# Graph attention with layer norm on one core: the move of transposed probabilities by groups of two slots, 128 KB an issue, from SyncE alone

## The reference

```
q, k, v = heads(x @ Wq + bq), heads(x @ Wk + bk), heads(x @ Wv + bv)
scores  = q @ k.T / 8
probs   = softmax(scores + where(adj, 0, -9e15))
ctx     = probs @ v                      # per head, then heads side by side
y       = x + ctx @ Wf + bf
out     = (y - mean(y)) / sqrt(var(y) + 1e-5)
```

## Time and profile before

| what | value |
|---|---|
| median of three runs | 1729.52 us (1724.23 to 1731.74) |
| the profiled execution, its own time | 1730.58 us |
| its span, first to last instruction | 1728.6 us |
| mean granted PE clock | 0.881 of 2.4 GHz |
| PE busy | 1326.2 us, 77% of the span |
| DVE busy | 1060.2 us, 61% |
| ACT busy | 721.8 us, 42% |
| POOL busy | 655.7 us, 38% |
| mean traffic of the DMA engines | 146 GB/s |

### The profile page before, as it was taken

One profiled execution on the slowest core, in us unless ns is written; L12 is line 12 of the kernel. 1 busy time (PEld: TensorE's weight loads), 2 busy tenths in 40 slices (PEclk: granted clock), 3 DMA queues, 4 the chain that ended last, 5 costly groups with the idle time before them and its releaser, 6 DMA issues.

```text
span 1728.6 us, 29185 instructions
## 1 busy us (share of the span) xinstructions
PE 1326.2 (77%) x8406; PEld 948.2 (55%) x8406; DVE 1060.2 (61%) x1617; ACT 721.8 (42%) x1404; POOL 655.7 (38%) x958
## 2 busy tenths in 40 slices
PE   7777887777877689677897688866887778888773
PEld 5555565545745457455574455644656545565542
DVE  5566665765656656565566765566656567566752
ACT  5444543444434444344443434434443435443430
POOL 2223542444414444154432543325433245333333
PEclk9888898889988889897998888988899889998877
DMA  4556655565455655555555555565555555555552
GB/s 152 141 132 154 159 143 147 150 160 153 121 152 147 163 147 131 147 150 155 147 136 152 149 151 141 138 156 152 149 145 138 154 153 150 153 133 153 149 144 74
DMA packets 184872, 251.61 MB, mean 146 GB/s; under 512 B 52464, under 2 KB 86384, under 8 KB 184688
## 3 DMA queue, kind: packets, MB, share of 16 engines
q1 hardware_dynamic: 147824, 199.06, 44.1%
q10 hardware_dynamic: 36864, 50.38, 11.9%
HBM read 35.33 MB, written 12.58 MB: 28 GB/s over the span
## 4 chain that ended last, share of the span: by engine, by line
SPq 79%; issue 9%; PE 4%; ACT 2%; DVE 2%; DMA 2%; ACTq 1%; POOL 1%; POOLq 0%; DVEq 0%
SPq L301 76%; PE context_ps L519 2%; DMA prob_t<-prob 1%; ACT prob L611 1%; DVE prob L697 1%; ACTq L301 1%; SPq L371 1%; PE score_ps L503 1%; SPq L357 1%; SPq L336 1%; SPq L364 1%; PE job_ps L408 0%; DMA x_in<-in_x_dram 0%; POOL res L294 0%; DVE weight_lo L758 0%
## 5 line engine op out<-in xcount | busy, mean ns | idle before, releaser
L519 PE MATMUL context_ps<-prob_t,v_all 128*64 128x256 f32 x3072 | 468.4, 472 | 239.8 <-DMA prob_t<-prob 239.8
L611 ACT ACTIVATE prob<-prob,row_min 128x1024 f32<-128x1024 f32 x384 | 439.5, 1146 | 500.1 <-DVE row_min L689 433.6
L689 DVE CUSTOM_DVE_ANT_0 prob<-score_ps,mask 128x1024 f32<-128x1024 f32 x384 | 454.3, 1220 | 206.1 <-PE score_ps L503 168.4
L697 DVE STREAM_TRANSPOSE prob<-prob 128x1024 f32<-128x1024 f32 x384 | 457.9, 1231 | 148.9 <-ACT prob L611 148.9
L519 PEld LDWEIGHTS context_ps<-prob_t,v_all 128*64 128x64 f32 x3072 | 294.6, 173 | 413.8 <-issue 298.3
L818 POOL TENSOR_TENSOR diag<-ident,inv_sum 128x512 f32<-128x512 f32 x96 | 99.9, 1040 | 410.5 <-DVE inv_sum L702 408.8
L619 ACT ACTIVATE context_hi<-context 128x256 fp32r<-128x256 f32 x96 | 40.1, 418 | 456.1 <-DVE context L707 285.2
L812 POOL TENSOR_TENSOR q_lo<-raw,q_hi 128x256 fp32r<-128x256 f32 x95 | 69.4, 730 | 351.0 <-ACT raw L603 350.9
L707 DVE TENSOR_TENSOR context<-context_ps,context 128x256 f32<-128x256 f32 x96 | 40.0, 416 | 238.1 <-PE context_ps L519 237.9
L408 PE MATMUL job_ps<-xt_hi,weight_hi 128*128 128x256 f32 (+1 forms) x423 | 149.4, 353 | 26.9 <-ACT raw L601 26.7
L503 PE MATMUL score_ps<-k_hi,q_hi 64*128 64x512 f32 x768 | 145.0, 456 | 21.8 <-DVE row_min L689 16.4
(11 more groups left out here) (72 smaller groups left out, 1717.7 us busy)
## 6 DMA issues: line engine op xcount, KB each, us to landing
prob_t<-prob SPq DMA_DIRECT2D x2304, 64.0 KB, 2.0
prob_t<-prob ACTq DMA_DIRECT2D x768, 64.0 KB, 2.1
res<-in_x_dram SPq DMA_DIRECT2D x32, 384.0 KB, 3.7
out_dram<-res SPq DMA_DIRECT2D x32, 384.0 KB, 2.5
x_in<-in_x_dram SPq DMA_DIRECT2D x30, 384.0 KB, 3.5
adj_in<-in_adj_dram SPq DMA_DIRECT2D x31, 256.0 KB, 2.8
prob_t<-in_L_gnn_Wk_dram SPq DMA_DIRECT2D x1, 576.0 KB, 3.9
prob_t<-in_L_gnn_Wq_dram SPq DMA_DIRECT2D x1, 576.0 KB, 7.8
```

The source lines that it names most:

```text
L519: last = pe.matmul(context_ps[64 * head:64 * head + 64, 0:GQ], v_all[:, kt, col:col + HS], keys, start=(kt == 0), stop=(kt == TT - 1))
L611: nc.scalar.activation(probabilities(t), probabilities(t), ACT.Exp, scale=-1.0, bias=row_min[:, ring:ring + 1], accum_out=row_sum[:, s // ...
L689: nc.vector.tensor_tensor_reduce(probabilities(t), in_quarters(score_ps[:, head, :]), in_quarters(mask[:, s % 2, :]), 1.0, HUGE, ALU.add, ...
L697: nc.vector.transpose(probabilities(t), probabilities(t)).then_inc(squared, 1)
```

## The change

A group is now moved at once, after its second slot. For each pair (a, c) one transfer carries the four units of the group, 128 KB in 32 runs of 4 KB. Sixteen issues a group stand on SP's queue. ACT issues none and no longer waits for the transposes. To make the runs contiguous, the layouts are `prob[P, group, c, slot, head, 256]` with two groups (before: three slots) and `prob_t[P, group, a, slot, head, 256]`. DVE waits for `landed` only in the first slot of a group, and for the group two before.

Other buffers become smaller: `res` has four tiles for eight, `context_hi` and `context_lo` four for six. The order changes with them: the mix of group g stands in slot 2g + 4 for g from 3 on (before: 2g + 3), mixes 0, 1 and 2 in slots 6, 8 and 9 (before 5, 6 and 7), the last two of a batch in the next one's slots 0 and 2. The p jobs, residuals, normalisations, loads and stores are placed anew, and the last batch has one more slot without units.

```diff
-RING = 3
 STEADY = {
-    0: [("k", 2, 0, 0), ("k", 2, 1, 0), ("p", -4, 0, 0)],
-    1: [("q", 2, 0, 0), ("i", -1, 0, 0), ("m", -1, 0, 0)],
-    2: [("p", -3, 0, 0), ("v", 0, 0, 0), ("v", 1, 0, 0)],
-    3: [("v", 2, 0, 0), ("v", 3, 0, 0), ("v", 4, 0, 0)],
-    4: [("q", 0, 1, 0), ("v", 5, 0, 0), ("v", 6, 0, 0), ("v", 7, 0, 0)],
-    5: [("i", 0, 0, 0), ("m", 0, 0, 0), ("q", 1, 1, 0)],
-    6: [("i", 1, 0, 0), ("m", 1, 0, 0)],
-    7: [("i", 2, 0, 0), ("m", 2, 0, 0)],
-    8: [("q", 2, 1, 0), ("p", -2, 0, 0), ("p", -1, 0, 0)],
-    9: [("i", 3, 0, 0), ("m", 3, 0, 0)],
...
+    0: [("q", 1, 0, 0), ("i", -2, 0, 0), ("m", -2, 0, 0)],
+    1: [("q", 2, 0, 0)],
+    2: [("i", -1, 0, 0), ("m", -1, 0, 0)],
+    3: [("v", 0, 0, 0), ("v", 1, 0, 0), ("v", 2, 0, 0)],
+    4: [("q", 0, 1, 0), ("q", 1, 1, 0), ("v", 3, 0, 0), ("v", 4, 0, 0)],
+    5: [("v", 5, 0, 0), ("v", 6, 0, 0), ("v", 7, 0, 0)],
+    6: [("i", 0, 0, 0), ("m", 0, 0, 0)],
+    7: [("q", 2, 1, 0), ("p", -2, 0, 0), ("p", -1, 0, 0)],
+    8: [("i", 1, 0, 0), ("m", 1, 0, 0)],
+    9: [("i", 2, 0, 0), ("m", 2, 0, 0)],
+    10: [("i", 3, 0, 0), ("m", 3, 0, 0)],
+    11: [("q", 0, 2, 0), ("x", 0, 0, 1), ("x", 1, 0, 1), ("x", 2, 0, 1), ("p", 0, 0, 0)],
+    12: [("i", 4, 0, 0), ("m", 4, 0, 0)],
+    13: [("q", 1, 2, 0), ("p", 1, 0, 0)],
+    14: [("i", 5, 0, 0), ("m", 5, 0, 0)],
+    15: [("q", 2, 2, 0), ("q", 0, 3, 0), ("p", 2, 0, 0)],
+    16: [("i", 6, 0, 0), ("m", 6, 0, 0)],
+    17: [("q", 1, 3, 0), ("q", 2, 3, 0), ("x", 0, 1, 1), ("x", 1, 1, 1), ("x", 2, 1, 1), ("p", 3, 0, 0)],
+    18: [("i", 7, 0, 0), ("m", 7, 0, 0)],
+    19: [("k", 0, 0, 1), ("k", 0, 1, 1)],
+    20: [("i", 8, 0, 0), ("m", 8, 0, 0)],
+    21: [("k", 1, 0, 1), ("k", 1, 1, 1), ("p", 4, 0, 0)],
+    22: [("q", 0, 0, 1), ("i", 9, 0, 0), ("m", 9, 0, 0)],
+    23: [("k", 2, 0, 1), ("k", 2, 1, 1), ("p", 5, 0, 0)],
 }
-STORES = {5: -2, 12: -1, 16: 0, 20: 1}
-RES_LOADS = {8: 2, 15: 3, 19: 0, 23: 1}
-X_LOADS = {2: (0, 0), 4: (0, 1), 11: (1, 0), 14: (1, 1)}
-RESIDUALS = {1: 0, 2: 1, 11: 2, 17: 3}
-NORMALISE = {3: -2, 10: -1, 13: 0, 18: 1}
+STORES = {4: -2, 10: -1, 16: 0, 20: 1}
+RES_LOADS = {8: 0, 12: 1, 18: 2, 22: 3}
+X_LOADS = {2: (0, 0), 4: (0, 1), 12: (1, 0), 14: (1, 1)}
+RESIDUALS = {2: -1, 10: 0, 14: 1, 20: 2}
+NORMALISE = {0: -2, 8: -1, 14: 0, 18: 1}
...
-        prob = sb("prob", [P, RING, 4, 2, GQ], F32)
-        prob_t = sb("prob_t", [P, 2, 2, 4, 2, GQ], F32)
+        prob = sb("prob", [P, 2, 4, 2, 2, GQ], F32)
+        prob_t = sb("prob_t", [P, 2, 4, 2, 2, GQ], F32)
...
-        def move_square(queue, s, a, c):
+        def move_square(queue, group, a, c):
-            group, qt, ring = s // 2, s % 2, s % RING
-            queue.dma_start(prob_t[32 * c:32 * c + 32, group % 2, qt, a].rearrange("p h n -> p (h n)"),
-                            prob[32 * a:32 * a + 32, ring, c].rearrange("p h n -> p (h n)")
-                            ).then_inc(landed[ring], 16)
+            queue.dma_start(prob_t[32 * c:32 * c + 32, group % 2, a].rearrange("p q h n -> p (q h n)"),
+                            prob[32 * a:32 * a + 32, group % 2, c].rearrange("p q h n -> p (q h n)")
+                            ).then_inc(landed[group % 2], 16)
...
-            def move(b, s):
-                sp.wait_ge(squared, at(b, UNITS, 2 * s + 2))
-                if s % 2 == 0:
-                    sp.sem_inc(sp_waited, 1)
-                    sp.wait_ge(mixed, at(b, GROUPS, s // 2 + 1))
+            def move(b, group):
+                sp.wait_ge(squared, at(b, UNITS, 4 * group + 4))
+                sp.sem_inc(sp_waited, 1)
+                sp.wait_ge(mixed, at(b, GROUPS, group + 1))
                 for a in range(4):
                     for c in range(4):
-                        if not (a == c):
-                            move_square(sp, s, a, c)
+                        move_square(sp, group, a, c)
...
                 for s in range(SLOTS):
-                    move(b, s)
+                    if s % 2 == 1:
+                        move(b, s // 2)
...
-            def move(b, s):
-                act.wait_ge(squared, at(b, UNITS, 2 * s + 2))
-                if s % 2 == 0:
-                    act.wait_ge(mixed, at(b, GROUPS, s // 2 + 1))
-                for a in range(4):
-                    for c in range(4):
-                        if a == c:
-                            move_square(act, s, a, c)
...
                 if head == 0:
-                    dve.wait_ge(landed[s % RING], at(b, 256 * SLOTS // RING, 256 * (s // RING + 1)))
+                    if s % 2 == 0:
+                        dve.wait_ge(landed[s // 2 % 2], at(b, 128 * GROUPS, 256 * (s // 4 + 1)))
```

More of the change, by code:

```diff
@@ L87, in slot_work @@
     if s >= SLOTS:
-        return LAST_24 if mode == "last" else []
+        return LAST_24 if s == SLOTS else LAST_25
     if mode == "first" and s < 2:
         return FIRST_0 if s == 0 else FIRST_1
-    if mode == "last" and s == 22:
-        return LAST_22
     return [w for w in STEADY[s] if not (mode == "first" and w[1] < 0) and not (mode == "last" and w[3] == 1)]
 def slots_of(mode):
-    return range(SLOTS + 1 if mode == "last" else SLOTS)
+    return range(SLOTS + 2 if mode == "last" else SLOTS)
 MODES = ("first", "mid", "last")
@@ L183, in graph_attention @@
         x_loaded = [sem(f"x_loaded{i}") for i in range(2)]
-        res_loaded = [sem(f"res_loaded{g}") for g in range(4)]
+        x_early = sem("x_early")
+        res_loaded = [sem(f"res_loaded{i}") for i in range(2)]
         adj_loaded = sem("adj_loaded")
@@ L190, in graph_attention @@
         squared = sem("squared")
-        landed = [sem(f"landed{i}") for i in range(RING)]
+        landed = [sem(f"landed{i}") for i in range(2)]
         inverted = sem("inverted")
@@ L213, in graph_attention @@
         pool_waited = sem("pool_waited")
-        stored = [sem(f"stored{g}") for g in range(4)]
+        stored = [sem(f"stored{i}") for i in range(2)]
         def at(b, per, plus):
@@ L284, in probabilities @@
         def probabilities(t):
-            return prob[:, t // 2 % RING, :, t % 2, :]
+            return prob[:, t // 4 % 2, :, t // 2 % 2, t % 2, :]
         def in_quarters(keys):
@@ L292, in scale_rows @@
             for tile in range(2):
-                n = (2 * group + tile) % TT
+                n = (2 * group + tile) % 4
                 engine.tensor_scalar(res[:, n, :], res[:, n, :], mean_var[:, group % 2, tile, 0:1],
@@ L327, in _ @@
             sp.dma_start(bf_rows[:], bf.partition_broadcast(P)).then_inc(bf_in, 16)
+            sp.wait_ge(job_done, 6)
             for g in range(2):
                 sp.dma_start(res[:, 2 * g:2 * g + 2, :], x_tiles[0, :, 2 * g:2 * g + 2, :]).then_inc(res_loaded[g], 16)
-            for i in range(RING):
-                sp.sem_inc(landed[i], 256)
+                sp.sem_inc(landed[g], 256)
             def load_adjacency(b, group):
@@ L382, in body @@
                         store(b, STORES[s])
[L383 to L388, removed]
+                    if s in RES_LOADS and (RES_LOADS[s] >= 2 or b.mode != "first"):
+                        load_residual(b, RES_LOADS[s])
             body(Batch("first", 0, 0))
@@ L396, in _ @@
                 store(last, group)
-            for g in range(4):
-                sp.wait_ge(stored[g], 16 * BATCH)
+            for i in range(2):
+                sp.wait_ge(stored[i], 32 * BATCH)
         @block.tensor
@@ L416, in transpose_x @@
                 for i in range(4):
-                    src = x_in[:, i] if mode != "start" or half == 0 else res[:, 4 + i]
+                    src = x_in[:, i] if mode != "start" or half == 0 else res[:, i]
                     last = pe.transpose(bank[:, i * P:(i + 1) * P], src[:, t * P:(t + 1) * P], ident[:])
@@ L463, in bank_free @@
                 if prior[0] == "p":
-                    assert not back
-                    pe.wait_ge(sum_done, at(b, TT, prior[1] + 9))
+                    pe.wait_ge(sum_done, at(b, TT, prior[1] + 9 - back * TT))
                 else:
@@ L509, in mix @@
                 pe.wait_ge(context_done, at(b, GROUPS, group + 2))
-                for s in (2 * group, 2 * group + 1):
-                    pe.wait_ge(landed[s % RING], at(b, 256 * SLOTS // RING, 256 * (s // RING + 2)))
+                pe.wait_ge(landed[group % 2], at(b, 128 * GROUPS, 256 * (group // 2 + 2)))
                 if group == 0:
@@ L538, in _ @@
                 if n == 3:
-                    for g in (2, 3):
-                        pe.wait_ge(res_loaded[g], 16)
+                    pe.wait_ge(x_early, 16)
                 if n >= 4:
@@ L713, in add_residual @@
                 dve.wait_ge(res_done, at(b, TT, n + 1))
-                nc.vector.tensor_tensor(res[:, n % TT, :], job_bank(b.mode, job)[:, 0:H], res[:, n % TT, :],
+                nc.vector.tensor_tensor(res[:, n % 4, :], job_bank(b.mode, job)[:, 0:H], res[:, n % 4, :],
                                         ALU.add).then_inc(sum_done, 1)
@@ L720, in moments @@
```

(17 more changed lines are left out.)

44 lines of the change are left out of this document (20 added, 24 removed), and 14 rows, old and new, of the table STEADY.

## The result

The changed kernel takes 1501.82 us in the median (1498.75 to 1508.24) against 1727.85 us for the kernel before in the same comparison. The ratio is 0.8696, with a 95% interval of 0.8657 to 0.8735. The forecast was 1490 us. The profiled execution has a span of 1506.3 us at a mean granted clock of 0.916.

The account below looks back on a forecast made before the run. SP's queue, issuing transfers, bounds the kernel. Slots' 161 us plus 6.2, 5.5, 1.3 and 5 make 179 a batch, taken as 180; 27 + 177 + 6 x 180 + 205.6, plus 2, gives about 1490 us (1400 to 1580).

Parts of the forecast that it names:

- Rival D: Whole kernel: nothing changes, as later mixes eat the saving or the chain was misread; 1730 us; 4 in 100.
- The price of an issue: SP's queue: an issue stays at 0.635 us with doubled bytes; a batch costs SP 130 us instead of 191.
- Rival C: SP's queue: an issue's time follows its bytes, 1.27 us each, 252 us a batch, about 2080 us; 4 in 100.
- rival A: DMA: the transfer becomes the limit at 160 GB/s, below the needed 206; a group lands after 15 us; 1570 us; 15 in 100.
- The new sum: Slot-by-slot walk of the new order plus delays: 179 us a batch, taken as 180.
- move(2) behind mix(0): Slot 8: group 2's transfer waits for a mix in slot 6, lands at 15.6 us and delays the slot by 1.3 us.
- diag(3) late: Slots 8 to 10: a normalisation on POOL delays the diagonal that i(3) needs; 22.6 us instead of 17.1, +5.5.
- q(2,2) late: Slot 15: POOL, busy normalising, makes q's low part late for slot 16's scores; slot takes 12.9 us, +6.2.
- other low clock: PE: lower clock after idling costs 2 us a batch outside slot 16, which has 3 us; slot 10's is counted elsewhere.
- Lateness on POOL: POOL works in order, so normalisations delay short jobs: +6.2 us at slot 15 and +5.5 us in slots 8 to 10.
- Rival B: POOL is not late and PE's clock stays up, so only 161 us a batch remain: about 1345 us; 13 in 100.
- the sum without lateness: All slots of a batch, before POOL's delays, the landing delay and low clock are added: 161 us.

Follow-up runs that it names:

- The halves: Changed kernel with each 128 KB transfer cut into two of 64 KB, all 32 a group on SP's queue: 2189.46 us, 1.2702 of the kernel before.
- the old counts in the new order: Changed kernel with 64 KB transfers, 24 a group on SP and 8 on ACT, as before the change: 1779.66 us, 1.0324 of the kernel before.

## Why the prediction was right, point by point

**The bound.** Right, and shown from both sides. SP's queue set the pace. The halves alone bring it back as the chain, at 1.27 of before, and the old counts in the new order land at 1.03. Rival D, no change, is out with the result.

**The price of an issue.** Right: 591 ns for 128 KB as for 64 KB. Rival C is out. A landing of 2.3 us was taken and 2.3 measured, so rival A is out at one queue's rate. It was not far off, though, as the last section tells.

**The new sum.** The first mask stands at 27.8 us (forecast 27). The first batch took 178.3 us (177), the six of the loop 182.5 on average (180), the last with the tail 205.1 (205.6). By slots, for the batch from 941.90 to 1123.26 us:

| slots | forecast, us | measured, us |
|---|---|---|
| 0 to 2 | 17.8 | 15.5 |
| 3 to 6 | 27.2 | 28.2 |
| 7 (move(2) behind mix(0)) | 9.9 | 10.1 |
| 8 to 10 (diag(3) late) | 22.6 | 22.0 |
| 11 | 9.1 | 10.7 |
| 12 | 5.7 | 5.6 |
| 13 | 7.4 | 10.0 |
| 14 | 5.7 | 5.7 |
| 15 (q(2,2) late) | 12.9 | 13.8 |
| 16 | 8.7 | 6.2 |
| 17 | 9.9 | 11.5 |
| 18 to 22 | 32.4 | 31.2 |
| 23 | 7.9 | 11.0 |
| other low clock | 2.0 | in the slots |
| batch | 179.2 | 181.4 |

The total is better than its terms: some came out 11.0 us longer in all and others 8.7 us shorter. That it was met within 2.2 us is in part luck. The batch shown is also a short one, by slot 10: the loop's other batches had 23.4 to 23.6 us in slots 8 to 10. Five terms deserve a word.

*Missed.* "The other buffers and semaphores cost nothing" was wrong. The ring of four context_hi places makes ACT wait for p(1), as the fourth row of the engines' waits shows. Slot 13 took 2.6 us more than forecast, and giving the places back made the changed kernel 1.1% faster.

*Missed.* The sum has DVE wait for a landing only before slot 8. In this batch it also waited before slots 4 (2.8 us) and 10 (2.2 us):

```profile
DVE prob L666 <- DMA prob_t<-prob: 6.8, 3, 2.8
```

So slot 3 took 7.9 us for 6.7 and slot 9 7.6 for 5.7. Of the 5.5 us that I booked as late diag(3), a part is this wait: moving normalise(-1) took 5.1 us from slots 8 to 10 on average over the loop of the profiled runs (23.3 to 18.2), and 3.0 us a batch from the whole by the ratios.

*Missed.* Slot 23 is 3.1 us longer. Its mask is preceded by a wait of 2.40 us that no engine explains:

```profile
1123.26 1.22 DVE L666 CUSTOM_DVE_ANT_0 prob<-score_ps,mask 128x1024 f32<-128x1024 f32 x1 [2.40 <-issue]
```

It stands at the loop's jump. The last slot of the first batch and of the loop's last pass took 8.5 us, those at the jump about 11. The kernel before has it as well, 3.5 us at 863.17, so it could have been read there. What the queue does there is not shown.

*Mis-sized.* PE's low clock. I booked the cost behind slot 15 as 3 us in slot 16 and 2 us in all other slots. It came instead inside slots 11, 13, 15 and 17, at granted clocks of 0.84, 0.83, 0.79 and 0.85, where p or the next scores run right after PE's wait for a copy or a low part. Slot 16 had 0.92. In the next batch slots 11 and 17 were at 1.00 and took 9.1 and 10.4 us (forecast 9.1 and 9.9).

*Mis-sized.* Slots 0 and 2 were priced by PE, 6.9 and 5.7 us, but PE had run ahead. Before slot 0 it did so while DVE stood at the jump: in the next batch its job q starts at 1120.64, 2.6 us before the mask. Before slot 2 it did so in slot 1, which DVE sets. So slots 0 to 2 went at DVE's pace of 5.0 to 5.3 us, and gave back 2.3 us of the excess. In the batches whose first mask has no wait at a jump, slot 0 took 6.0 and 6.1 us.

**Lateness on POOL.** Right in place and size: 6.2 us were forecast for slot 15, and moving the normalisation took 6.6 from it, with 54 us in the run. Rival B, at 1345 us, asked for these delays to be absent. They were real: with both of them and the context wait removed the kernel reaches 1396 us, and 1373 with p ahead of x. At 1396 us a batch of the loop takes 168 us on average, where the sum without lateness had 161, or 164 with the 1.3 for move(2) and 2 of low clock. So that part of the sum was too low, and the total hid it.

**ACT.** I wrote that taking the issues from ACT "takes nothing off the path by itself". For the kernel before no run shows it. In the new order it is wrong, if ACT's waits stand in front of the next exponentials: 71 us. The issues themselves cost nothing measurable.

**Issue against transfer.** The Trainium skill holds that the sequencer's time to start a DMA is usually small beside the DMA itself (page "DMA: Bandwidth & Descriptors", section "Issuing engines are not separate DMA queues"). This kernel is the other case. An issue of 591 ns is short beside a landing of 2.0 to 2.3 us, but landings overlap and the issues of one queue do not. The halves move the same bytes and cost 688 us more.

## What to carry to other kernels

When the chain that ended last is a queue that issues transfers, count its issues and make each carry more; an issue's time did not depend on its bytes here. Then walk the new order slot by slot, since the next bound is made of single late items: a long job placed ahead of a short one that another engine needs, a ring made smaller, a wait for a later slot's work in front of work that is due. Whether an issue may stand on a busy engine depends on what its wait holds up, not on its own half microsecond.

## What the runs showed of the hardware that I had not expected

Landing depended on the size of the pieces and on how many queues issued them at once. With 64 KB pieces the median was 2.0 us, from one queue (the halves on SP) as from two. With 128 KB from one queue it was 2.3 us, and with 128 KB from two queues 3.0 and 3.6 us. The stretches below are of the changed kernel.

```profile
1054.00:1059.00 5.00, 0.00 (x0) 0.00 (x0) 2.04 (x5) 0.85 (x3) 4.06 (x9) 0.87 0.88 247
```

```profile
1057.00:1062.00 5.00, 1.68 (x8) 1.40 (x10) 0.00 (x0) 0.00 (x0) 3.95 (x4) 0.57 0.91 207
```

In the first the DMA engines were busy 0.88 of the time and moved 247 GB/s, but a load of x (384 KB, issued at 1053.30) has a part in it. In the second only pieces of the move are issued. They make 207 GB/s, the 206 that the prediction needs, and the engines are already busy 0.91. So one queue with 128 KB an issue nearly fills them while it issues. That fits the longer landings with two queues, and pieces of 256 KB would probably find the engines, not the queue, as what sets the landing of a group (argued, not run).
